# A four-layer graph network on one core: the gather of the next step is interleaved with the projection of this one

## The reference

```
h = relu(layernorm(x))
layer 0: x += elu( softmax_over_nodes(mask(leaky(Wh1 + Wh2'), adj > 0.5)) @ (h W0) )
layer 1: x += relu( D (adj + I) D h W1 + bias ),   D = 1/sqrt(row sums)
layer 2: x += relu( adj h W2 ) * (row of h is not all zero)
layer 3: x += relu( h W3a + (adj h / row sum of adj) W3b )
```

## Time and profile before

| | |
|---|---|
| median of 3 runs | 2551.06 us (2551.01 to 2554.61) |
| the profiled execution | 2552.76 us |
| its span, first to last instruction | 2551.0 us |
| PE busy | 2483.8 us, 97% of the span |
| DVE busy | 2016.9 us, 79% |
| ACT busy | 1398.7 us, 55% |
| POOL busy | 1232.7 us, 48% |
| mean granted TensorE clock | 0.993 |

### The profile page before, as it was taken

One profiled execution on the slowest core, in us unless ns is written; L12 is line 12 of the kernel. 1 busy time (PEld: TensorE's weight loads), 2 busy tenths in 40 slices (PEclk: granted clock), 3 DMA queues, 4 the chain that ended last, 5 costly groups with the idle time before them and its releaser, 6 DMA issues.

```text
span 2551.0 us, 40561 instructions
## 1 busy us (share of the span) xinstructions
PE 2483.8 (97%) x13098; PEld 2144.6 (84%) x13098; DVE 2016.9 (79%) x4373; ACT 1398.7 (55%) x2571; POOL 1232.7 (48%) x1607
## 2 busy tenths in 40 slices
PE   4799999999999999999999999999999999999998
PEld 3678888888888888888888888888888888888887
DVE  7788888878788888878788888888888878878853
ACT  4455555555555555556556555555555555555542
POOL 3455544544544544544544455445455455455431
PEclk9899999999999999999999999999999999999999
DMA  3112222222222221222222222222222222222210
GB/s 132 50 44 53 59 67 52 59 67 51 60 67 51 60 67 50 61 66 50 62 62 54 60 63 55 63 57 58 60 60 57 60 61 57 61 61 56 49 34 25
DMA packets 355314, 149.15 MB, mean 58 GB/s; under 512 B 279200, under 2 KB 319520, under 8 KB 355104
## 3 DMA queue, kind: packets, MB, share of 16 engines
q1 hardware_dynamic: 355104, 146.56, 23.2%
HBM read 80.87 MB, written 33.61 MB: 45 GB/s over the span
## 4 chain that ended last, share of the span: by engine, by line
PE 91%; DVE 3%; POOL 2%; SPq 1%; issue 1%; DMA 1%; ACT 1%; POOLq 0%; ACTq 0%; DVEq 0%
PE O L358 44%; PE T L358 34%; PE X L358 13%; SPq L302 1%; DVE ln_stats L702 1%; POOL h_lo L998 0%; DMA wh_dram<-wh 0%; DVE dump L718 0%; POOL ln_scale L983 0%; ACT h L499 0%; DMA wh_rows<-wh_dram 0%; DVE t_lo L764 0%; DMA xs<-x 0%; POOL xs L968 0%; DVE act_out L795 0%
## 5 line engine op out<-in xcount | busy, mean ns | idle before, releaser
L998 POOL TENSOR_TENSOR h_lo<-h,h_hi 128x512 fp32r<-128x512 f32 x384 | 539.9, 1428 | 360.0 <-ACT h_hi L505 359.7
L499 ACT ACTIVATE h<-xs,ln_bias,ln_scale 128x512 f32<-128x512 f32 x512 | 396.0, 811 | 438.4 <-POOL ln_bias L991 435.6
L358 PE MATMUL O<-w_hi,t_hi 128*128 128x512 f32 x1536 | 598.2, 389 | 0.8 <-DVE t_lo L764 0.8
L358 PE MATMUL O<-w_lo,t_hi 128*128 128x512 f32 x1536 | 597.8, 389 | 0.0
L358 PE MATMUL O<-w_hi,t_lo 128*128 128x512 f32 x1536 | 597.7, 389 | 0.0
L764 DVE TENSOR_TENSOR t_lo<-T,t_hi 128x512 fp32r<-128x512 f32 x512 | 347.1, 688 | 254.9 <-ACT t_hi L511 254.7
L511 ACT CAST t_hi<-T 128x512 fp32r<-128x512 f32 x512 | 298.3, 583 | 419.7 <-PE T L358 419.7
L962 POOL TENSOR_TENSOR xs<-xs,act_out 128x512 f32<-128x512 f32 x128 | 164.4, 1305 | 565.3 <-ACT act_out L539 561.5
L702 DVE BATCH_NORM_STATS2 ln_stats<-xs 128x6 f32<-128x512 f32 x512 | 328.4, 679 | 17.8 <-POOL xs L968 17.5
L358 PEld LDWEIGHTS O<-w_hi,t_lo 128*128 128x128 f32 x1536 | 288.5, 188 | 60.0
L358 PEld LDWEIGHTS O<-w_hi,t_hi 128*128 128x128 f32 x1536 | 288.7, 188 | 56.3 <-DVE t_lo L764 1.4
(11 more groups left out here) (96 smaller groups left out, 5040.4 us busy)
## 6 DMA issues: line engine op xcount, KB each, us to landing
xs<-x SPq DMA_DIRECT2D x64, 512.0 KB, 5.1
out<-xs SPq DMA_DIRECT2D x64, 512.0 KB, 4.5
h<-act_out SPq DMA_DIRECT2D x976, 32.0 KB, 1.9
a_raw<-adj_t SPq DMA_DIRECT2D x64, 256.0 KB, 2.7
a_rows<-adj SPq DMA_DIRECT2D x64, 256.0 KB, 2.7
wh_rows<-wh_dram SPq DMA_DIRECT2D x59, 128.0 KB, 4.2
z<-w_all SPq DMA_DIRECT2D x3, 512.0 KB, 3.6
xs<-w_all SPq DMA_DIRECT2D x3, 512.0 KB, 10.3
```

Of the source, the lines that this page charges most:

```text
L358: last = nc.tensor.matmul(psum, s, m, start=(start and n == 0 and i == 0), stop=(stop and n == len(pairs) - 1 and i == 2))
L499: nc.scalar.activation(h[:, k.odd, m], xs[:, k.xb, m], ACT.Relu, bias=ln_bias[:, k.quad, m:m + 1], scale=ln_scale[:, k.quad, m:m + 1], acc ...
L998: nc.gpsimd.tensor_tensor(h_lo[:, k.odd, m], h[:, k.odd, m], h_hi[:, k.odd, m].bitcast(F32), ALU.subtract).then_inc(h_lo_ready, 1)
```

## The change

A new function on PE, `gather_and_project(new, k)`, does the whole gather of step j + 1 and the whole projection of step j in one piece of program. The n = 0 half of the projection is woven into the gather: two products into T, one into O, and so on through all four blocks f. The n = 1 half follows in one piece. The function is used where step j + 1 is of layer 1 or 2 and step j of layer 0 or 1, from slot 10 on, so in slots A and B of every round; slots C and D are as before. The programs of the other engines are untouched. The products are the same 48, on the same operands.

```diff
+            def gather_and_project(new, k):
+                a, t, w, c = new.ab, k.odd, k.layer, slice(0, P)
+                wait(pe, h_hi_ready, new.done(L012))
+                ...
+                o_free(pe, k, 0)
+                for f in range(FT):
+                    u = slice(f * P, f * P + P)
+                    first, second = [(h_hi[:, new.odd, m, u], h_lo[:, new.odd, m, u]) for m in range(NT)]
+                    if f % HALF == 0:
+                        t_free(new, f // HALF)
+                        pe.wait_ge(t_lo_ready, k.part(ALL, NT, f // HALF))
+                    if f == 0:
+                        pe.wait_ge(h_lo_ready, new.part(L012, NT, 0))
+                    nc.tensor.matmul(T[:, f], first[0], a_hi[:, a, 0], start=True, stop=False)
+                    nc.tensor.matmul(T[:, f], first[0], a_lo[:, a, 0], start=False, stop=False)
+                    nc.tensor.matmul(O[:, t, 0], t_hi[:, t, f, c], w_hi[:, w, f], start=f == 0, stop=False)
+                    nc.tensor.matmul(T[:, f], first[1], a_hi[:, a, 0], start=False, stop=False)
+                    if f == 0:
+                        pe.wait_ge(h_lo_ready, new.part(L012, NT, 1))
+                    nc.tensor.matmul(T[:, f], second[0], a_hi[:, a, 1], start=False, stop=False)
+                    nc.tensor.matmul(O[:, t, 0], t_hi[:, t, f, c], w_lo[:, w, f], start=False, stop=False)
+                    nc.tensor.matmul(T[:, f], second[0], a_lo[:, a, 1], start=False, stop=False)
+                    gathered = nc.tensor.matmul(T[:, f], second[1], a_hi[:, a, 1], start=False, stop=True)
+                    if f % HALF == HALF - 1:
+                        gathered.then_inc(t_ready, 1)
+                    projected = nc.tensor.matmul(O[:, t, 0], t_lo[:, t, f, c], w_hi[:, w, f], start=False, stop=f == FT - 1)
+                projected.then_inc(o_ready, 1)
+                o_free(pe, k, 1)
+                product(O[:, t, 1], [...]).then_inc(o_ready, 1)
...
-                gather_step(step(j + 1))
+                mixed = j > FILL and step(j + 1).layer in (1, 2) and step(j).layer in (0, 1)
+                if mixed:
+                    gather_and_project(step(j + 1), step(j))
+                else:
+                    gather_step(step(j + 1))
...
-                if j not in PROJECT_FIRST:
+                if j not in PROJECT_FIRST and not mixed:
                     project_step(step(j))
```

More of the change, by code:

```diff
@@ L442, in project @@
                     last.then_inc(o_ready, 1)
+            def gather_and_project(new, k):
+                a, t, w, c = new.ab, k.odd, k.layer, slice(0, P)
+                wait(pe, h_hi_ready, new.done(L012))
+                if new.layer == 1:
+                    pe.wait_ge(ah_lo_ready, new.done(L1, 2))
+                if new.layer == 2:
+                    pe.wait_ge(a_lo_ready, new.done(L2))
+                o_free(pe, k, 0)
[22 more added lines that the diff above has]
+                o_free(pe, k, 1)
+                product(O[:, t, 1], [(t_hi[:, t, f, P:N], t_lo[:, t, f, P:N], w_hi[:, w, f], w_lo[:, w, f])
+                                     for f in range(FT)]).then_inc(o_ready, 1)
             def gather_last(k):
```

## The result

| | before | after |
|---|---|---|
| median of 6 runs | 2552.96 us | 2629.94 us (2629.57 to 2631.85) |
| ratio | | 1.0309, 95% interval 1.0298 to 1.0319 |
| span of the profiled execution | 2551.0 us | 2628.8 us |
| a round, start to start, in the steady middle | 38.433 us | 39.800 us |

The kernel is 77 us slower; the forecast was 2628. (One of the six runs of before was a stray of 14 ms; the ratio leaves it out.)

The account below looks back on a forecast made before the run. PE alone, full in the middle, was taken as the bound. 60 rounds x 1.29 us of new stall = 77 us, on the profiled 2552.76 gives 2630; the median 1.7 lower, so 2628 us; 8 in 10: 2585 to 2655.

Parts of the forecast that it names:

- T half 1 comes 2.49 us later into the slot: Slots A and B: last T product starts 5.20 us into the slot, behind 23 T and 11 O, against 2.71 before.
- the room of 1.44 us: Start of slot C: before the change, ht_lo half 1 was done 1.44 us before PE wanted it.
- The stall's size, 1.29 us: Each slot C: PE waits for ht_lo, 1.05 us plain (2.49 - 1.44) and 0.24 for restarting.
- the restart: Slot C: PE starts 0.16 us after the ht_lo it waits for, next product 0.08 late; 0.24 us.
- The weaving costs 0: Slots A and B: each product costs its own length whatever its neighbour; 0, with 0.65 us a round allowed either way.
- Slot A costs nothing: Slot A: DVE work ends 2.49 us later, but nothing on PE needs it and the dots' DMA stays hidden; cost 0.
- 60 rounds at 1.29 us: Whole run: 61 carried steps of layer 3, the last waiting for DMAs anyway, so 60 rounds pay; 77 us.
- (a): Slots A and B: same stall, but weaving saves or costs 0.65 us a round; 2589 or 2667 us; chance 7%.
- (b): Slot C: POOL and DVE no longer meet, stall nearly vanishes to 0.26 us a round; 2567 us; chance 7%.
- (c): Slot D: second stall through p_lo and t_lo, 0.6 us more a round; 2665 us; chance 9%.
- (d): Slots A and B: woven products run faster, at 0.025 us saved each 2520 us; chance 3%.
- (e): After each new gap the clock falls, 1.8 us a round, 108 us on top, 2736 us; chance 1%.

Follow-up runs that it names:

- f1_ht_first: Changed kernel with ht_hi and ht_lo of slot B put ahead of T half 1 on ACT and DVE; 2561.25 us against 2555.84.
- e5_five: Changed kernel with only 5 of the 12 O products woven in ahead of the last T product; 2555.46 us against 2554.78 before the change.
- e6_eight: Changed kernel with only 8 of the 12 O products woven in ahead of the last T product; 2584.25 us, ratio 1.0117.
- f4_block: Changed kernel with the 36 products in blocks (12 T, 11 O, 12 T, 1 O), not alternated; 2623.86 us against 2555.84.
- g4_ht_first_grouped: Changed kernel with ht_hi and ht_lo ahead of T half 1, woven as six T, three O, four times; 2556.16 us, ratio 0.9999.
- f3_slot_b: Changed kernel with only slot B woven; 2623.49 us against 2555.84, ratio 1.0263.
- g1_short_h_lo: Changed kernel with POOL making layer 0's h_lo for 8 of 512 columns, from graph 4 on; 2574.31 us against 2556.61.
- e7_no_meeting: Changed kernel with POOL's h_lo of layer 0 moved behind the normalisation that follows it; 2624.83 us, ratio 1.0285.
- g2_slot_a_short_h_lo: Changed kernel with only slot A woven and layer 0's h_lo made for 8 of 512 columns; 2559.00 us against 2556.61.
- f2_slot_a: Changed kernel with only slot A woven; 2569.53 us against 2555.84, ratio 1.0051.

## Why the prediction was right

**PE was full, so only waits could matter.** Right: the round grew by waits of 1.19 us and by 0.19 us of products.

**T half 1 comes 2.49 us later into the slot.** Right: `t_hi` half 1 starts 5.57 us into slot B (1214.99, slot start 1209.42), where 5.51 was forecast; the 0.06 are the slower woven products.

**The chain `t_hi`, `h_hi`, `ht_hi`, `ht_lo`, and the room of 1.44 us.** Right, shown three ways: cut, the stall goes (`f1_ht_first`); with a delay of 1.13 us it is not there, with 1.81 it is, at the size that the room gives (`e5_five`, `e6_eight`); without any weaving it stays (`f4_block`).

**The stall's size, 1.29 us.** It is 1.19 us. One term that was too large is the restart, forecast at 0.24: I had charged the second start with the 0.16 us of latency and 0.08 us on top. The seventh product starts 0.05 us behind `ht_lo` half 1 (1217.07 + 3.06 = 1220.13, start at 1220.18) and the eighth comes 0.11 late: 0.16 in all. In `f4_block`, where nothing else plays in, the stall is 1.23 us. The rest is an overlap that the sum did not have: the weaving makes slot B 0.09 us longer, and T half 1 comes only 0.05 us later by it (its last T product starts 5.25 us into the slot, and 5.20 in `f4_block`). PE asks for `ht_lo` later by more than `ht_lo` is delayed, so 0.04 to 0.05 us of the stall are covered.

**The weaving costs 0.** Wrong by 0.19 us a round, well inside the 0.65 allowed. The argument from neighbourships held for blocks (`f4_block`, `g4_ht_first_grouped` cost 0.000) and failed for two T products and one O in turn, which the trace of before does not have.

**Slot A costs nothing.** True of the stall in the full change, for a reason I did not give: slot B's delay covers it (`f3_slot_b` has the same stall). Alone it costs 0.25 us of stall, since late DVE work meets POOL. My sum took the delays one slot at a time and kept DVE's durations as they were; that was safe only for `ht_lo`.

**No second stall at slot D, clock unchanged.** Right: no wait in slots C and D in the table, 1.00 in the windows. The room left there is as forecast: `t_lo` half 0 of slot C ends 0.96 us before PE starts slot D, where "some 0.9" was worked out.

**60 rounds at 1.29 us.** The two errors of size, 0.10 too much and 0.19 too little, nearly cancelled: 1.37 us a round. That the time came within 2 us of the forecast is therefore in part luck. And 60 x 1.37 would be 82 us, and the spans differ by 77.8. The starts of `project_first` tell why: 55 rounds of the steady middle, 298.83 to 2412.64 before, 303.20 to 2492.19 after, bring 75.2 us; the first rounds bring 4.4, the round after the middle 0.6. The very end gives back: 0.7 us in the last three rounds, and from the last `project_first` to the end of the span are 21.0 us before and 19.4 after, at a granted clock of 0.92 and 0.99 in the last 39 us, which the change did not cause by anything I can show.

**The rivals.** (a) A cost of the weaving is real, a quarter of what I had allowed. (b) POOL and DVE still meet; `g1_short_h_lo` shows what it would have been, 0.24 us of stall, as worked out there (0.26). (c) did not happen, but it took only `e7_no_meeting`'s swap to bring it about, and `g2_slot_a_short_h_lo` and `g4_ht_first_grouped` have it in some rounds. (d) and (e) did not happen.

## What to carry to other kernels

When PE is full, reordering its products has no wait to take away, and none of the orders tried here gained. Ask first when each result becomes available and what stands in program order behind the instruction that picks it up. Measure the room of each such chain, not the idle share of its engine: ACT was idle 45% of the time here and DVE 21%, and the room was 1.44 us. And when work on DVE moves in time, its durations move too, if POOL runs beside it.

## What the runs showed of the hardware that I had not expected

- A DVE instruction that did not slow down in its old place can do so a microsecond later: `mask_add`, with one SBUF input, took 1.22 us beside POOL's xs (`f2_slot_a`) and 0.42 us in the kernels before and after, where POOL did not run beside it.
- Single O products of 512 columns behind each second T product of 256 take 0.233 us, not 0.227, and the twelve O products behind such a stretch 0.04 us more together, most of it in the first nine; in groups of three among six there is no excess, nor for single ones behind each third T product (`e6_eight`). All this is shown, the cause is not; it stays open.
- The first product of slot C, waiting, starts 0.15 us behind the end of `ht_lo` half 0 and the next comes 0.08 us late; the seventh starts 0.05 us behind half 1 and the next comes 0.11 us late. In `g1_short_h_lo` `ht_lo` half 0 is done at 1230.95, 0.01 us before PE would start at 1230.97 (1230.74 + 0.227), and PE still starts at 1231.10 and runs the next product 0.08 us late: data that come just in time cost a wait of 0.13 us and the 0.08.

```profile
1230.26 1.29 DVE L818 TENSOR_TENSOR ht_lo<-h,ht_hi 128x512 fp32r<-128x512 f32 x2 [0.44 <-ACT ht_hi L559]
...
1230.74 0.39 PE L358 MATMUL O<-w_hi,t_lo 128*128 128x512 f32 x1
1231.10 0.47 PE L358 MATMUL T<-w_hi,ht_hi 128*128 128x512 f32 x1
1231.41 0.39 PE L358 MATMUL T<-w_lo,ht_hi 128*128 128x512 f32 x1
```
